# Key-padding mask in the attention scores: part of it moved from a TensorE product to a GpSimd word product

## The chip, the cores and the metric

One core of a Trainium2 chip runs the whole program. The number that counts is device time in microseconds (us) of one execution. TensorE is called PE here, VectorE DVE, ScalarE ACT, GpSimd POOL; the DMA queue of SyncE is SP.

## What is computed

The input is `x` of 8 sequences of 512 tokens by 256 features. Three residual blocks follow each other. The first is a bidirectional Mamba with a feed-forward. The second, the one that matters here, is cross attention with 16 heads of 16 features over 512 keys, of which the last ones are padding and are masked for every query. The third is a feed-forward whose result goes through five steps of a spiking neuron.

```python
scores = jnp.einsum('bhqd,bhkd->bhqk', q, k) / math.sqrt(D_HEAD)
scores = jnp.where(mask == 0, jnp.float32(-1000000000.0), scores)
attn = jax.nn.softmax(scores, axis=-1)
out = jnp.einsum('bhqk,bhkd->bhqd', attn, v)
...
y = jnp.einsum('bsf,df->bsd', h, W_proj)
def step(mem, _):
    reset = jax.lax.stop_gradient(spike_fn(mem - THRESHOLD))
    mem_new = BETA * mem + y - reset * THRESHOLD
```

## The kernel before

There are two passes. `mamba_pass` takes the first 1700 us or so and is not touched by the change. `attention_pass` then goes through the eight sequences (batches), and each engine has its own program, written out by hand, with semaphores between them. What stands in one engine's program stays in that order.

One batch on PE is, in this order: the first half of the feed-forward of the next batch (`up`, `down`) interleaved with `prescore` (scores whose maximum per query DVE takes, the line of `masked`); then the attention proper; then key, value, output and query projections; then the spiking feed-forward (`fc`, `spike_input`).

The attention proper works with transposed scores: keys lie on partitions, queries along the free axis. It has eight **units** (0 to 7). Unit `u` is a group of four heads (`g = u // 2`) and two of the four key tiles (`2s` and `2s + 1` with `s = u % 2`). A unit has two **halves**, each with two heads. `score(b, unit, half)` makes, for each of its two heads and each of the unit's two key tiles, two bf16 products of 512 columns into one PSUM bank: `k_st` by `q_st` (L1411 and L1412), and then `ident_bf` by `mask_biasT`, which adds minus 2^32 to the scores of the padded keys. So a half has eight products. The two banks of a head form a `pair` tile, of which there are two, so a head waits for the exponential of the head two places earlier. ACT takes the exponential of a pair, 128 by 1024, into `pr`. `weigh(b, unit, half)` multiplies one key tile of `pr` of four heads by `v_sb` (with a column of ones, for the softmax sum); half 0 takes key tile `2s`, half 1 takes key tile `2s + 1`. PE's order is

```python
for unit in range(H // 2):
    for half in range(2):
        if unit + 1 < H // 2:
            score(b, unit + 1, half)
        weigh(b, unit, half, it)
    if unit % 2 == 0 and unit > 0:
        to_tokens(unit // 2 - 1, it)
```

with `score(b, 0, 0)` and `score(b, 0, 1)` ahead of the loop. In the traces a weigh reads as eight MATMUL records (each fp32 product is two), and `to_tokens` is the transposes from `oT` at L1435.

Meanwhile DVE adds the feed-forward's result to `x1n` (L1671), runs the five spike steps of the batch before (`cnt`, `tmp`, `mem`, 128 by 1024 fp32, L1718 to L1737), with the query norm of the next batch between step 1 and step 2 (statistics L1635 and L1642, application L1649), and after each `to_tokens` a `normalise` (L1702, L1706). POOL's program in a batch is short: `x1n` sums, the cutting of the maxima into three bf16 parts (L1892 to L1898), `rstd_of` of the query norm and of the later norm (L1863, L1865), another sum. It has nothing to do during the attention's units.

Of the kernel before, what the change touches and what calls it, by code (L numbers as in the profile page):

```python
# [11 lines left out]
B, T, D = 8, 512, 256  # L12
DI, NS, RK, CW = 512, 16, 16, 4
FF = 1024
H, DH = 16, 16
P = 128
# [6 lines left out]
QR = 6 * DH + 3  # L23
# [17 lines left out]
_cols()  # L41


Q_PART = [0, 0, 1, 0, 2, 1]
K_PART = [0, 1, 0, 2, 0, 1]

# [1057 lines left out]
def attention_pass(nc, ctx, a, mid, out, sb, where, stage, psum, consts, handover, early):  # L1104

    f32, bf16, i32 = mybir.dt.float32, mybir.dt.bfloat16, mybir.dt.int32
    ALU, ACT, AX = mybir.AluOpType, mybir.ActivationFunctionType, mybir.AxisListType
    ident, cols, minus_half, col, settle, s_const = consts
    pair, bank, y_bank, general = psum
# [26 lines left out]
    v_sb = sb("v_sb", [P, TT, H, 32])  # L1136
    qk = sb("qk", [P, 2, KD, T])
    qk_part = sb("qk_part", [P, 2, 3, KD, T], bf16)
    oT = sb("oT", [P, 2, T])
    m_col = sb("m_col", [P, TT, H])  # L1140
    m_part = sb("m_part", [H // 2, 2, 3, T], bf16)
    m_rest = sb("m_rest", [H // 2, T])
# [53 lines left out]
    m_cut = stage("m_cut", ahead=1)  # L1196
    s_sc = stage("score")
    s_exp = stage("exp", ahead=2)
    g_out = stage("g_out")
    out_ready = stage("out_ready")  # L1200

    with nc.Block() as block:
# [96 lines left out]
        def _(pe):  # L1299
            pe.wait_ge(handover.sem, handover.count(0))  # L1300

            def mm(o, lhsT, rhs, start=True, stop=True):
                return pe.matmul(o, lhsT, rhs, start=start, stop=stop)  # L1303
# [96 lines left out]
            def score(b, unit, half):  # L1400

                g, s = unit // 2, unit % 2
                if unit == H // 4 and half == 0:
                    pe.wait_ge(s_mr[1].sem, s_mr[1].count(b))
                for hh in (2 * half, 2 * half + 1):
                    hd = 4 * g + hh
                    n = b * 2 * H + unit * 4 + hh
                    pe.wait_ge(s_exp.sem, s_exp.count(n - 2))
                    for t in range(2):
                        kt = 2 * s + t  # L1410
                        mm(pair[hh % 2][:, t, :], k_st[0:QR, hd, kt * P:(kt + 1) * P], q_st[0:QR, hd, :], True, False)  # L1411
                        last = mm(pair[hh % 2][:, t, :], ident_bf[:, :], mask_biasT[:, kt, :], False, True)  # L1412
                    last.then_inc(s_sc.sem, 1)

            def weigh(b, unit, half, it):

                g, s = unit // 2, unit % 2
                pe.wait_ge(s_exp.sem, s_exp.count(b * 2 * H + unit * 4 + 3))
                key = ("av", g)
                if s == 0 and half == 0:  # L1420
                    pe.wait_ge(*G.free(key, it))
                bk = G.bank(key, it)
                kt = 2 * s + half
                for hh in range(4):
                    last = mm(bk[32 * hh:32 * hh + 32, :], v_sb[:, kt, 4 * g + hh, :], pr[:, hh, kt, :],
                              kt == 0, kt == TT - 1)
                if kt == TT - 1:
                    last.then_inc(G.full_sem(key), 1)
# [195 lines left out]
        def _(dve):  # L1624
# [6 lines left out]
            def norm_stats(n, src):  # L1631

                dve.drain()
                for j in range(TT):
                    dve.bn_stats(stats[:, j, :], src[:, j, :])  # L1635
                norm_mean(n)
# [28 lines left out]
            def add_down(beta, it):  # L1665

                dve.wait_ge(x1n_set.sem, x1n_set.count(beta))
                for jj in range(TT // 2):
                    dve.wait_ge(*G.full(("w2", jj), it))
                    bk = G.bank(("w2", jj), it)  # L1670
                    dve.tensor_tensor(two(x1n, jj), two(x1n, jj), bank_tiles(bk), ALU.add).then_inc(G.done_sem(("w2", jj)), 1)  # L1671
# [17 lines left out]
            def take_q(it):  # L1689
                for m in range(KD):  # L1690
                    dve.wait_ge(*G.full(("q", m), it))
                    bk = G.bank(("q", m), it)
                    dve.scalar_tensor_tensor(qk[:, 1, m, :], bk[:, :], col("bq", m), not_full[:, :],
                                                              ALU.add, ALU.mult).then_inc(G.done_sem(("q", m)), 1)
# [63 lines left out]
            for jj in range(TT // 2):  # L1758
                take_v(jj, BEFORE)
            dve.drain()  # L1760
            dve.tensor_tensor(mask_biasT[:, :, :], keep[:, :, :],
                              not_full[:, :].unsqueeze(1).broadcast_to((P, TT, T)), ALU.mult)
            take_q(BEFORE)
            cut_lo(0, 1)
            cut_last(0, 1)
# [18 lines left out]
            def batch(b, it, more):  # L1784
# [7 lines left out]
                start, step, finish = spikes(b)  # L1792
                if more:
                    add_down(b + 1, it)
                start()
                step(1)
                if more:
                    norm_stats(ATT, x1n)
                    norm_apply(ATT, b + 1, x1n, xn_q)
                step(2)  # L1800
                normalise(0, it)
# [54 lines left out]
        def _(pool):  # L1856
# [47 lines left out]
            rstd_of(FF1, 1)  # L1904
            take_x1(0)

            def batch(b, more):
                if more:
                    start_x1n(b + 1)
                for i in range(2):  # L1910
                    cut_maxima(b, i)
                if more:
                    rstd_of(ATT, b + 1)
                rstd_of(FF2, b)
                if more:
                    pool.wait_ge(kinds["wo"][1].sem, kinds["wo"][1].count(2 * b + 1))
                    take_x1(b + 1)
                    rstd_of(FF1, b + 2)
# [131 lines left out]
```

## Time and profile before

| | us |
|---|---|
| median of 3 runs | 2940.82 (2939.02 to 2941.04) |
| the profiled execution's own time | 2934.87 |
| its span in the trace | 2933.1 |
| PE busy | 2739.0 (93%) |
| PE weight loads busy | 1812.9 (62%) |
| DVE busy | 2189.3 (75%) |
| ACT busy | 1757.3 (60%) |
| POOL busy | 1554.4 (53%) |

The shares mix two passes. The page's 40 slices show them apart: up to about 1700 us POOL is busy at 80 to 90%, afterwards at 10 to 20%, while PE stays at 90% or more. Matmul records overlap, so a busy PE says only that it had work in hand; how fast it goes is read from the starts of its records.

### The profile page before, as it was taken

Reading aid. Unit: us, or ns where it says so; the run is one execution under the profiler, and the core shown is the slowest. Engines: PE = TensorE matmul, PEld = TensorE weight load, DVE = VectorE, ACT = ScalarE, POOL = GpSimd, SP = SyncE. Lnnn points to the kernel's source line nnn. Section 1 sums busy time; section 2 is a strip of 40 time slices with the busy share of each in tenths; the row PEclk is TensorE's granted clock in tenths of the full one; section 3 lists DMA queues with packets and bytes.
Section 4 is the critical chain, followed back from the end, with each engine's and each line's share of the span. In section 5 each row is a group of like instructions: output and inputs, shape, how many; then the busy total and the mean of one; then the engine's idle time right before and its main releaser. Section 6 shows DMA issues by size and latency. Waiting matters only on the chain. (4 is left out here: it accounts for less than half of the span.)

```text
span 2933.1 us, 55353 instructions
## 1 busy us (share of the span) xinstructions
PE 2739.0 (93%) x19289; PEld 1812.9 (62%) x19330; DVE 2189.3 (75%) x3270; ACT 1757.3 (60%) x2899; POOL 1554.4 (53%) x850
## 2 busy tenths in 40 slices
PE   5999999999999999999999868999999999999996
PEld 2777777777777777777777744454454545454523
DVE  3988888888889888888888857474748484747473
ACT  5778877877877777678778423535344444444332
POOL 1888888888888888888889821111111111111010
PEclk9999999999999999999999989999999999999978
DMA  3122111202211221212122062414140505050400
GB/s 115 31 75 77 59 62 61 98 26 74 83 63 52 75 77 48 73 61 90 34 73 96 8 142 60 67 28 68 27 73 22 83 11 93 2 93 2 79 2 15
DMA packets 113355, 174.50 MB, mean 59 GB/s; under 512 B 15233, under 2 KB 88065, under 8 KB 113057
## 3 DMA queue, kind: packets, MB, share of 16 engines
q1 hardware_dynamic: 113104, 171.34, 22.9%
q8 instruction: 136, 2.23, 0.3%
q14 instruction: 115, 0.93, 0.1%
HBM read 148.38 MB, written 22.94 MB: 58 GB/s over the span
## 5 line engine op out<-in xcount | busy, mean ns | idle before, releaser
L1066 POOL TENSOR_TENSOR hC<-h,C_rep 128x1024 f32<-128x1024 f32 x512 | 1203.8, 2365 | 236.2 <-PE y_bank L538 231.3
L924 DVE TENSOR_TENSOR_SCAN h<-dA,pair 128x512 f32<-128x512 f32 x1024 | 1178.2, 1203 | 159.4 <-PE pair L447 144.6
L677 ACT ACTIVATE dA<-delta,cols 128x511 f32<-128x511 f32 x1024 | 664.6, 710 | 99.5 <-DVE h L924 93.7
L447 PEld LDWEIGHTS pair<-diagB,duT 64*128 64x128 f32 x8192 | 497.8, 187 | 236.3 <-issue 185.0
L447 PE MATMUL pair<-diagB,duT 64*128 64x128 f32 x8192 | 595.9, 285 | 17.9 <-issue 9.0
L538 PE MATMUL y_bank<-ident,hC 128*128 128x128 f32 x4120 | 563.4, 280 | 13.5 <-POOL hC L1066 11.7
L538 PEld LDWEIGHTS y_bank<-ident,hC 128*128 128x128 f32 x4120 | 441.9, 141 | 79.7 <-POOL hC L1066 19.6
L1790 DVE CUSTOM_DVE_ANT_0 masked<-pair,mask_bias 128x512 f32<-128x512 f32 x512 | 321.9, 687 | 27.5 <-PE pair L1303 13.8
L1863 POOL TENSOR_SCALAR rstd<-mv 128x4 f32<-128x4 f32 x24 | 11.6, 484 | 563.7 <-DVE mv L1642 563.7
L1535 ACT ACTIVATE pr<-pair 128x1024 f32<-128x1024 f32 x256 | 248.3, 1021 | 94.1 <-PE pair L1303 84.0
L447 PE MATMUL general<-xnT,w_in 128*128 128x512 f32 x512 | 252.4, 604 | 7.3 <-ACT zs L677 5.1
L1303 PE MATMUL general<-w_down,g 128*128 128x256 f32 x1024 | 232.5, 380 | 2.8 <-DVEq L1627 2.8
L1892 POOL CAST m_part<-m_rest 8x512 bf16<-8x512 f32 x16 | 12.1, 754 | 417.5 <-ACT m_rest L1535 417.5
L1303 PEld LDWEIGHTS general<-w_down,g 128*128 128x128 f32 x1024 | 193.7, 190 | 34.9 <-issue 3.8
L1303 PE MATMUL pair<-q_st,k_st 99*128 99x512 bf16 x512 | 196.4, 384 | 13.6 <-ACT pr L1535 11.1
L1303 PE MATMUL general<-xT,w_up 128*128 128x512 f32 x360 | 184.0, 652 | 5.9 <-ACT xT L1535 5.5
L1303 PE MATMUL pair<-mask_biasT,ident_bf 128*128 128x512 bf16 x472 | 179.7, 381 | 0.0
L1303 PE MATMUL pair<-k_st,q_st 96*128 96x512 bf16 x512 | 150.6, 403 | 17.3 <-DMA q_st<-qk_parts 13.7
L934 DVE SCALAR_TENSOR_TENSOR u<-general,cols,u 128x511 f32<-128x511 f32 (+2 forms) x192 | 141.0, 734 | 26.6 <-ACT u L677 23.2
L1702 DVE RECIPROCAL rsum<-general 128x16 f32<-128x16 f32 x32 | 8.2, 258 | 192.1 <-PE general L1435 192.1
L1303 PEld LDWEIGHTS pair<-q_st,k_st 99*128 99x128 bf16 x512 | 50.2, 98 | 143.5 <-ACT pr L1535 97.8
L1303 PEld LDWEIGHTS general<-xT,w_up 128*128 128x128 f32 x360 | 74.1, 210 | 85.5 <-issue 74.8
(173 smaller groups left out, 3161.1 us busy)
## 6 DMA issues: line engine op xcount, KB each, us to landing
C_rep<-c_rows SPq DMA_DIRECT2D x128, 512.0 KB, 3.7
w_in<-w_in SPq DMA_DIRECT2D x16, 1024.0 KB, 4.9
qk_parts<-qk_part SPq DMA_DIRECT2D x48, 256.0 KB, 2.5
k_st<-qk_parts SPq DMA_DIRECT2D x48, 256.0 KB, 8.9
q_st<-qk_parts SPq DMA_DIRECT2D x48, 256.0 KB, 8.9
x_in<-x SPq DMA_DIRECT2D x18, 512.0 KB, 4.3
w_out<-w_out SPq DMA_DIRECT2D x17, 512.0 KB, 4.4
mid<-x_out SPq DMA_DIRECT2D x9, 512.0 KB, 6.5
```

What stands on the lines that cost most here:

```text
L447: return pe.matmul(o, lhsT, rhs, start=start, stop=stop)
L538: last = pe.matmul(y_bank[:, c * P:(c + 1) * P], hC[:, g % 2, i, c * P:(c + 1) * P], ident[:, :], start=j == 0 and i == 0 and c == 0, stop ...
L677: return act.activation(o, i, fn, **kw)
L924: last = dve.tensor_tensor_scan(h[:, g % 4, i, :], dA[:, g % 4, i, :], dBu[:, i, :], 0.0, ALU.mult, ALU.add)
L934: dve.scalar_tensor_tensor(u[n][:, k, lag:T], raw[:, 0:T - lag], col("fb"[n] + "conv_w", CW * k + CW - 1 - lag), u[n][:, k, lag:T], ALU.mu ...
L1066: pool.tensor_tensor(hC[:, g % 2], h[:, g % 4], C_rep[:, 2 * j:2 * j + 2, :], ALU.mult).then_inc(s_hC.sem, 1)
L1303: return pe.matmul(o, lhsT, rhs, start=start, stop=stop)
L1535: return act.activation(o, i, fn, **kw)
L1702: dve.reciprocal(rsum[:, :, :], o[:, :, :, DH:DH + 1].squeeze(3))
L1790: dve.tensor_tensor_reduce(masked[:, j % 2, :], bank[j], mask_bias[:, j, :], 1.0, FLOOR, ALU.add, ALU.max, m_col[:, j, hd:hd + 1]).then_in ...
L1863: pool.tensor_scalar(rstd[:, :], mv[:, :, 1], EPS, None, ALU.add)
L1892: pool.tensor_copy(high, m_rest[:, :])
```

## The change

For units 1 to 7, the second head of each half (heads 1 and 3 of the group, the table `ON_POOL`) has no mask product in the second of its two key tiles. The exponentials there are then those of unmasked scores. POOL multiplies them afterwards, in place, as 32-bit integer words by `keep_word`, which is 1 for a kept key and 0 for a padded one: one `TENSOR_TENSOR` of 128 by 512 for each half of units 1 to 7, 14 a batch and 112 in all. It waits for the exponential of its head, and `weigh` of half 1 now waits for POOL's second product of its unit in place of the exponential. `keep_word` is made once by DVE, after `mask_biasT`. It takes the place in memory of `oT`, and `oT` becomes the tile `xT[1]`, which is in use only later in a batch. DVE takes the statistics of the query norm before the first spike step and not after step 1, since POOL's `rstd_of` for them stands ahead of its word products.

```diff
+ON_POOL = ((1,), (3,))
...
-    oT = sb("oT", [P, 2, T])
+    oT = xT[1]
+    keep_word = sb("keep_word", [P, 2, T], i32)
...
+                        on_pool = unit > 0 and t == 1 and hh in ON_POOL[half]
+                        last = mm(pair[hh % 2][:, t, :], k_st[0:QR, hd, kt * P:(kt + 1) * P], q_st[0:QR, hd, :], True, on_pool)
+                        if not on_pool:
+                            last = mm(pair[hh % 2][:, t, :], ident_bf[:, :], mask_biasT[:, kt, :], False, True)
...
-                pe.wait_ge(s_exp.sem, s_exp.count(b * 2 * H + unit * 4 + 3))
+                if half == 0 or unit == 0:
+                    pe.wait_ge(s_exp.sem, s_exp.count(b * 2 * H + unit * 4 + 3))
+                else:
+                    pe.wait_ge(s_kept.sem, s_kept.count(b * (H - 2) + unit * 2 - 1))
...
+            dve.drain()
+            dve.tensor_scalar(keep_word[:, :, :], mask_biasT[:, 1::2, :], 0.0, None, ALU.is_equal).then_inc(s_word.sem, 1)
...
                     add_down(b + 1, it)
+                    norm_stats(ATT, x1n)
                 start()
                 step(1)
                 if more:
-                    norm_stats(ATT, x1n)
                     norm_apply(ATT, b + 1, x1n, xn_q)
...
+            def mask_exp(b, unit, half):
+
+                kt = 2 * (unit % 2) + 1
+                heads = ON_POOL[half]
+                pool.wait_ge(s_exp.sem, s_exp.count(b * 2 * H + unit * 4 + heads[-1]))
+                settle(pool)
+                words = pr[:, heads[0]:heads[-1] + 1, kt, :].bitcast(i32)
+                pool.tensor_tensor(words, words, keep_word[:, unit % 2, :].unsqueeze(1).broadcast_to((P, len(heads), T)),
+                                   ALU.mult).then_inc(s_kept.sem, 1)
+
+            pool.wait_ge(s_word.sem, s_word.count(0))
...
                 if more:
                     rstd_of(ATT, b + 1)
+                for unit in range(1, H // 2):
+                    for half in range(2):
+                        mask_exp(b, unit, half)
                 rstd_of(FF2, b)
```

PE, one half: the score of unit 2, half 1 and the weigh of unit 1, half 1 behind it. Before:

```order
L1408 REGISTER_ALU
L1303 MATMUL pair<-q_st,k_st 128x512 [waits exp]
L1303 MATMUL pair<-mask_biasT,ident_bf 128x512
L1303 MATMUL pair<-q_st,k_st 128x512
L1303 MATMUL pair<-mask_biasT,ident_bf 128x512
L1303 MATMUL general<-pr,v_sb 32x512 [waits exp]
L1303 MATMUL general<-pr,v_sb 32x512 x3
```

These rows are the half's second head and the weigh. The same place after:

```order
L1412 REGISTER_ALU
L1307 MATMUL pair<-q_st,k_st 128x512 [waits exp]
L1307 MATMUL pair<-mask_biasT,ident_bf 128x512
L1307 MATMUL pair<-q_st,k_st 128x512
L1427 ISA
L1307 MATMUL general<-pr,v_sb 32x512 [waits masked_exp]
L1307 MATMUL general<-pr,v_sb 32x512 x3
```

The head's second mask product is gone, and the weigh waits for POOL's `masked_exp`, not for ACT's `exp`.

POOL, from the cutting of the second half of the maxima to the rstd of the later norm. Before:

```order
L1896 CAST m_part<-m_rest 8x512
L1898 TENSOR_TENSOR m_part<-m_rest,m_part 8x512
L1863 TENSOR_SCALAR rstd_7300<-mv_7299 128x4 [waits ln1_stats]
L1865 TENSOR_TENSOR rstd_7300<-rstd_7300,minus_half 128x4
L1861 REGISTER_ALU
L1863 TENSOR_SCALAR rstd_7300<-mv_7299 128x4 [waits ln2_stats]
```

After, where the pair of rows from L1922 on stands 14 times:

```order
L1907 CAST m_part<-m_rest 8x512
L1909 TENSOR_TENSOR m_part<-m_rest,m_part 8x512
L1874 TENSOR_SCALAR rstd_7300<-mv_7299 128x4 [waits ln1_stats]
L1876 TENSOR_TENSOR rstd_7300<-rstd_7300,minus_half 128x4
L1922 ISA
L1925 TENSOR_TENSOR pr<-pr,keep_word 128x512 [waits exp]
```

The word products stand between the two norms' rstd.

DVE, from the sum into `x1n` to the query norm's application. Before:

```order
L1671 TENSOR_TENSOR x1n<-x1n,general 128x512 [waits w2_full]
L1718 TENSOR_SCALAR cnt<-y_sb 128x1024 [waits out_dma]
L1724 SCALAR_TENSOR_TENSOR tmp<-y_sb 128x1024
L1726 SCALAR_TENSOR_TENSOR mem<-y_sb,tmp 128x1024
L1732 SCALAR_TENSOR_TENSOR cnt<-mem,cnt 128x1024
L1635 BN_STATS stats_7298<-x1n 128x6 x4
L1642 BN_AGGR mv_7299<-stats_7298 128x2 x4
L1649 TENSOR_SCALAR xn_q<-x1n,mv_7299,rstd_7300 128x256 [waits ln1_rstd]
```

After:

```order
L1680 TENSOR_TENSOR x1n<-x1n,general 128x512 [waits w2_full]
L1644 BN_STATS stats_7298<-x1n 128x6 x4
L1651 BN_AGGR mv_7299<-stats_7298 128x2 x4
L1727 TENSOR_SCALAR cnt<-y_sb 128x1024 [waits out_dma]
L1733 SCALAR_TENSOR_TENSOR tmp<-y_sb 128x1024
L1735 SCALAR_TENSOR_TENSOR mem<-y_sb,tmp 128x1024
L1741 SCALAR_TENSOR_TENSOR cnt<-mem,cnt 128x1024
L1658 TENSOR_SCALAR xn_q<-x1n,mv_7299,rstd_7300 128x256 [waits ln1_rstd]
```

The statistics have moved ahead of the four instructions of the spike steps.

## Rows read from the trace of the kernel before

**Rows 1.** The page: busy tenths of an engine in 40 slices of the span

```profile
PE   5999999999999999999999868999999999999996
...
POOL 1888888888888888888889821111111111111010
```

**Rows 2.** Groups by line, PE, 1800 to 2933: count, busy, mean ns, idle before

```profile
L1303 PE MATMUL pair<-mask_biasT,ident_bf 128*128 128x512 bf16 x472 | 179.7, 381 | 0.0
```

**Rows 3.** Timeline, second batch, units 1 to 3: start, duration, engine

```profile
1969.98 0.39 PE L1303 MATMUL pair<-q_st,k_st 99*128 99x512 bf16 x1
1970.20 0.38 PE L1303 MATMUL pair<-mask_biasT,ident_bf 128*128 128x512 bf16 x1
...
1971.06 1.94 ACT L1535 ACTIVATE pr<-pair 128x1024 f32<-128x1024 f32 x2 [0.91 <-PE pair L1303]
...
1971.52 0.38 PE L1303 MATMUL pair<-mask_biasT,ident_bf 128*128 128x512 bf16 x1
...
1971.82 1.06 PE L1303 MATMUL general<-pr,v_sb 128*32 128x512 f32 x8
...
1977.52 1.07 PE L1303 MATMUL y_bank<-pr,v_sb 128*32 128x512 f32 x8
```

**Rows 4.** Timeline, second batch, the first scores of unit 1

```profile
1962.31 0.10 PEld L1303 LDWEIGHTS pair<-q_st,k_st 99*128 99x128 bf16 x1 [0.37 <-ACT pr L1535]
...
1962.47 1.94 ACT L1535 ACTIVATE pr<-pair 128x1024 f32<-128x1024 f32 x2 [0.22 <-PE pair L1303]
```

**Rows 5.** Timeline, second batch, POOL and DVE: alone, and side by side

```profile
1938.60 1.15 POOL L1894 TENSOR_TENSOR m_rest<-m_rest,m_part 8x512 f32<-8x512 f32 x1
1939.88 0.60 POOL L1896 CAST m_part<-m_rest 8x512 bf16<-8x512 f32 x1
...
1958.09 1.95 POOL L1894 TENSOR_TENSOR m_rest<-m_rest,m_part 8x512 f32<-8x512 f32 x1
...
1959.11 2.01 DVE L1726 SCALAR_TENSOR_TENSOR mem<-y_sb,tmp 128x1024 f32<-128x1024 f32 x1
...
1969.02 1.23 DVE L1730 SCALAR_TENSOR_TENSOR mem<-mem,tmp 128x1024 f32<-128x1024 f32 x1
```

**Rows 6.** Groups by line, POOL, 1750 to 2933

```profile
L1875 POOL TENSOR_TENSOR x1n<-x_in,x_mid 128x1024 f32<-128x1024 f32 x7 | 16.5, 2351 | 4.3 <-issue 4.3
```

**Rows 7.** Timeline, second batch, from the last scores to the key projection

```profile
1999.40 0.39 PE L1303 MATMUL pair<-q_st,k_st 99*128 99x512 bf16 x1
...
2000.48 1.94 ACT L1535 ACTIVATE pr<-pair 128x1024 f32<-128x1024 f32 x2 [0.91 <-PE pair L1303]
...
2002.83 1.92 PE L1303 MATMUL y_bank<-pr,v_sb 128*32 128x512 f32 x16
...
2004.69 0.30 PEld L1303 LDWEIGHTS general<-ctxT,w_att 128*128 128x128 f32 x2 [0.84 <-issue]
```

**Rows 8.** Timeline, second batch, DVE between the transposes; ACT's key projection

```profile
1991.07 0.26 DVE L1702 RECIPROCAL rsum<-general 128x16 f32<-128x16 f32 x1 [6.74 <-PE general L1435]
...
1996.01 1.23 DVE L1737 SCALAR_TENSOR_TENSOR tmp<-cnt,x_res 128x1024 f32<-128x1024 f32 x1
...
2002.94 0.26 DVE L1702 RECIPROCAL rsum<-general 128x16 f32<-128x16 f32 x1 [5.70 <-PE general L1435]
...
2006.71 0.69 ACT L1535 ACTIVATE qk<-general,cols 128x512 f32<-128x512 f32 x1 [1.29 <-PE general L1303]
```

**Rows 9.** Timeline, before the first batch, DVE: what follows the mask tile

```profile
1734.01 0.75 DVE L1693 SCALAR_TENSOR_TENSOR qk<-general,cols,not_full 128x512 f32<-128x512 f32 x1 [0.39 <-PE general L1303]
1736.19 0.75 DVE L1693 SCALAR_TENSOR_TENSOR qk<-general,cols,not_full 128x512 f32<-128x512 f32 x1 [1.44 <-PE general L1303]
```

**Rows 10.** Stretches of 10 us; the number before the DMA share is PE's clock

```profile
2020.00:2030.00 10.00, 6.55 (x16) 2.88 (x15) 5.35 (x7) 1.60 (x3) 2.62 (x2) 0.75 0.93 163
2030.00:2040.00 10.00, 10.00 (x23) 4.29 (x22) 4.24 (x10) 8.33 (x13) 0.00 (x0) 0.91 0.80 110
...
2170.00:2180.00 10.00, 9.31 (x21) 4.13 (x21) 2.48 (x3) 5.91 (x10) 0.00 (x0) 0.83 1.15 126
```

More of the change, by code:

```diff
@@ L1198, in attention_pass @@
     s_exp = stage("exp", ahead=2)
+    s_kept = stage("masked_exp")
+    s_word = stage("mask_words")
     g_out = stage("g_out")
@@ L1410, in score @@
                         kt = 2 * s + t
-                        mm(pair[hh % 2][:, t, :], k_st[0:QR, hd, kt * P:(kt + 1) * P], q_st[0:QR, hd, :], True, False)
-                        last = mm(pair[hh % 2][:, t, :], ident_bf[:, :], mask_biasT[:, kt, :], False, True)
+                        on_pool = unit > 0 and t == 1 and hh in ON_POOL[half]
+                        last = mm(pair[hh % 2][:, t, :], k_st[0:QR, hd, kt * P:(kt + 1) * P], q_st[0:QR, hd, :], True, on_pool)
+                        if not on_pool:
+                            last = mm(pair[hh % 2][:, t, :], ident_bf[:, :], mask_biasT[:, kt, :], False, True)
                     last.then_inc(s_sc.sem, 1)
```

## The prediction

> **What bounds the kernel now.** I read the page's slices first. After the Mamba pass PE is busy at nine tenths while POOL falls to one tenth [rows 1]. That suggests that PE sets the pace and POOL is free, but busy shares do not prove it, so I went to the timeline of one batch. There the attention's halves follow each other without a hole on PE. In [rows 3] weighs start at 1971.82 and, two halves later, at 1977.52: a half takes 2.85 us. The scores ahead of the first of them start at 1969.98, so 1.84 of it are eight products, and 1.01 the weigh. ACT needs 1.94 us for the two exponentials of a half and stands idle 0.91 until PE has given it a new pair [rows 3]. So PE is the bound, and ACT has room. The eight batches go alike, unit for unit.
>
> The price of one mask product must be read from starts. From 1970.20 to 1971.52 six products start, 0.22 us apart [rows 3], while the same records read 381 ns each [rows 2], because they overlap. Taken at 381 ns, 112 products would be 43 us; at the pitch they are 24.6. I use the pitch. The Trainium skill says the same (Trainium Kernel Development and Optimization, Performance Expectations): matmul busy time is a poor metric, since matmuls are pipelined. That sentence excludes the sum of 43, and the trace agrees.
>
> **What is removed.** 14 mask products a batch, 112 in all: 112 x 0.22 = 24.6 us, if all of it lies on the path. In the steady halves it does: each half goes from 2.85 to 2.63 us. Can ACT follow? A half's first head keeps its four products, so its exponential still starts 1.08 us after the scores (1971.06 less 1969.98), and the pair ends at +3.02. The next half's first head needs the first exponential, ended near +2.10, at +2.63. Its second head comes at +3.51 and needs the second, ended at +3.02. 0.5 us are left, so ACT does not become the bound. In unit 1 PE does wait for exponentials: the fourth head's end releases the second head of unit 1 at 1962.31 [rows 4]. But what is taken away there comes behind that wait and directly ahead of the next weigh, and the first head, whose products start the exponential of 1962.47, keeps all four. So it counts too.
>
> **What is added on POOL.** 14 products a batch of 128 by 512 words. No integer product is in the trace. The nearest rows are two-input operations: 2.35 us for 128 by 1024 fp32 [rows 6], so half, 1.18, for 512; and 1.15 for 8 by 512 when DVE leaves POOL alone [rows 5]. A lower bound is the 0.60 of a one-input cast of 512 [rows 5]; an upper one is 2.35, as if a word cost what two floats cost. I take 1.18, as the two-input rows agree on it whatever their type in or out.
>
> POOL must be ready for the weigh of half 1. Take the scores that start at 1969.98 (unit 2, half 1). Their exponentials end at 1973.00, and the weigh that reads the second key tile starts at 1977.52 [rows 3], 4.52 us later. Three products fewer lie before it now, so 3.86. POOL needs some 0.16 to start, 1.18 to run and 0.05 to release PE: 1.4. This is hidden, with 2.5 to spare. Only one POOL product falls in each 2.63 us, so it keeps pace.
>
> At the **end of unit 7** there is no next score to hide behind. The last scores start at 1999.40, call it S, and the exponentials end at 2002.42, S + 3.02. The two last weighs start at 2002.83 and take 1.86 together until 2004.69 [rows 7], the second at half of that. With one product fewer the first starts at S + 3.21 and the second would at S + 4.14. POOL is done at 3.02 + 1.4 = S + 4.42. PE waits 0.28 a batch, 8 x 0.28 = 2.2 us. With a POOL product of 0.60 this is nothing; with 2.35 it is 1.45 a batch, 11.6 in all.
>
> **DVE and POOL disturb each other.** Side by side, POOL's 1.15 becomes 1.95 and DVE's 1.23 becomes 2.01 [rows 5]; each row reads as if one had stood still until the other was done. The Trainium skill has that as a rule (SBUF — State Buffer, two separate sides): the port pair is an exclusive lock, and a DVE operation with two SBUF inputs and a GpSimd one that reads SBUF exclude each other. So a word product can wait up to 1.23 for a spike step: 1.4 + 1.23 = 2.6 of the 3.86 us, still hidden. The other way round, about four word products fall between two transposes of the outputs and can hold DVE up by 4 x 1.18 = 4.7 us; that stretch also becomes 0.9 shorter. DVE was idle 6.74 and 5.70 us before its two later reciprocals [rows 8], so 5.6 still fits, barely. Its last step of a batch, 1996.01 to 1997.24, would end at worst near 2002, still ahead of the last word product (near 2002.6 on the old scale), so I leave that one undisturbed. The ACT work that waits for that step's DMA starts at 2006.71 [rows 8], 9.5 us after the step, against a delay of 4.7 and a DMA of 512 KB. Cost: nothing.
>
> **The statistics' move** costs nothing. It adds no instruction on DVE, only an order, and the spike steps that come later by it have the idle time just named behind them. POOL's rstd then waits for POOL's own cutting of the maxima alone. Of the cutting, two operations of at most 1.95 are left when the one of 1958.09 ends at 1960.04 [rows 5]; with 2 us for the rstd, an estimate from the same rows for two operations, POOL is free by 1966. The first word product's exponential ends at 1964.41 [rows 4], and the weigh that wants it and the next one was at 1971.82 and is now near 1970.9. Two word products at 2.6 fit ahead of that, if DVE disturbs no more than one of them fully. What follows on POOL's queue, the later norm's rstd, waits for the output projection, which comes behind the last weigh anyway. SP's queue keeps its order. PE's new wait brings one register instruction for each weigh of half 1, hidden while its array works.
>
> **keep_word**, once: 128 by 1024 on DVE, up to 1.2 us after a drain, behind the mask tile. DVE's next instruction starts at 1734.01 after a wait of 0.39, the one behind it, at 1736.19, waits 1.44 for PE [rows 9]. With 1.2 us from 1733.77 on, the first ends at 1735.7, before the second can start. The size of 1.2 is from the spike steps, 1.23 for 128 by 1024 [rows 5]. Cost 0; uncovered, it would be 1.2.
>
> **The sum.** 24.6 - 2.2 = 22.4 us. The profiled execution took 2934.87, and would take 2912.5. The median of the runs, 2940.82, lies 6 above it; I carry the difference over: **2918.4 us**.
>
> **PE's clock** adds noise. After each attention PE idles for the later norm and then shows half clock, 1.2 instead of 2.4 GHz, for a while. In the stretches of 10 us the loss is 0.25 + 0.09 of 10 us, 3.4, in one batch, and 0.17, 1.7, in the next [rows 10]. Five of eight batches show the long form, three the short. As the batch gets shorter, which batches draw which may change: 5 us more if all were long, 8.5 less if all were short. I allow 4 either way.
>
> **Rivals.**
> (a) *The last word product is late*, either since an integer product costs more (1.6 to 2.6 us) or since DVE still holds it up by 1.23. For it: no integer row, and a margin on DVE of only half a microsecond. Against: the steady two-input rows. 1.2 us a batch, 9.6 in all: 2928. The skill's GPSIMD Engine Reference (When to use GPSIMD) says that only a 32-bit integer add has a native path and that the ordinary one computes in fp32; by that the product would go at the fp32 rate and this rival falls. No row here shows it.
> (b) *POOL becomes the bound, slower than before.* 14 products with a gap of 0.15 must fit between the first exponential, near 1964.6, and the last weigh, near 2003.8: 39.2 us, 2.8 each. From 2.65 us a product on, the kernel loses. At 3.0 it is 14 x 3.15 = 44.1, so 4.9 a batch and 39 in all: 2980. Nothing in the rows goes as slowly.
> (c) *The products come off but the halves stay at 2.84*, because the wait of a head for the exponential two places back decides after all. This would need 0.5 us more in that loop than the rows show: 2941.
>
> **How the numbers follow.** Forecast 0.70; (a) 0.14; (b) 0.07; (c) 0.04; 0.05 for a gain above the 24.6, by the clock. The range goes from 2911 (all 24.6 gained, nearly all of it with 4 to 5 us of clock) to 2931 (rival (a) with a worse clock). A measurement of this kernel can tell about 0.2%, 6 us, from no change. Faster by more 0.88, within 0.05, slower 0.07.
>
> **What would show it.** In the changed kernel the starts of weighs in the steady halves lie 2.63 apart; POOL shows 112 word products of about 1.2 us, some near 2 beside a spike step; ACT's idle time before a pair falls from 0.91 to about 0.7; the last weigh waits about 0.3 us for POOL. From the first pair of exponentials of unit 1 to the last pair of unit 7 (1962.47 to 2000.48) it is 38.0 us now; 13 products fewer lie between, so it should be 35.2. Wrong would be: word products above 2.6 us, weighs of half 1 that wait for POOL in every unit, or a gap that grows behind the attention.

## The result, and the profile after

The changed kernel took 2918.03 us (median of 4 runs, 2916.24 to 2921.48) beside 2939.92 of the kernel before (4 runs, 2938.96 to 2941.04). By the medians that is 21.9 us faster. The ratio is 0.9927, with a 95% interval of 0.9912 to 0.9941, or 17 to 26 us. Forecast were 2918.4 us, 22.4 us faster. The profiled execution took 2919.11 us, with a span of 2917.3.

The page of after shows POOL's slices, which answer to [rows 1], and two groups by line (operation, shapes, count | busy us, mean ns | idle before):

```profile
POOL 1788888888888888888889821323232322223130
...
L1544 ACT ACTIVATE pr<-pair 128x1024 f32<-128x1024 f32 x256 | 248.4, 1021 | 72.4 <-PE pair L1307 72.1
...
L1925 POOL TENSOR_TENSOR pr<-pr,keep_word 128x512 int32<-128x512 int32 x112 | 156.4, 1396 | 131.3 <-ACT pr L1544 128.2
```

POOL has gone from one tenth to two or three in the attention. It spends nearly as long waiting for exponentials (128.2 us) as at work (156.4): it keeps up.

The next view is the timeline of the second batch of after (start, duration, engine), unit 1 to unit 3; it answers to [rows 3] and [rows 4]:

```profile
1964.07 1.94 ACT L1544 ACTIVATE pr<-pair 128x1024 f32<-128x1024 f32 x2 [0.22 <-PE pair L1307]
...
1967.28 1.28 POOL L1925 TENSOR_TENSOR pr<-pr,keep_word 128x512 int32<-128x512 int32 x1 [0.41 <-issue]
...
1972.54 1.07 PE L1307 MATMUL general<-pr,v_sb 128*32 128x512 f32 x8
...
1975.16 1.07 PE L1307 MATMUL y_bank<-pr,v_sb 128*32 128x512 f32 x8
...
1977.24 1.94 ACT L1544 ACTIVATE pr<-pair 128x1024 f32<-128x1024 f32 x2 [0.69 <-PE pair L1307]
...
1977.79 1.06 PE L1307 MATMUL y_bank<-pr,v_sb 128*32 128x512 f32 x8
```

Weighs start at 1972.54, 1975.16 and 1977.79: a half now takes 2.62 to 2.63 us where it took 2.85. ACT's idle time ahead of a pair is 0.69 where it was 0.91. Both differences are 0.22, one mask product.

The end of the same batch, which answers to [rows 7] and [rows 8]:

```profile
1990.47 0.26 DVE L1711 RECIPROCAL rsum<-general 128x16 f32<-128x16 f32 x1 [5.21 <-PE general L1444]
...
1993.46 1.71 POOL L1925 TENSOR_TENSOR pr<-pr,keep_word 128x512 int32<-128x512 int32 x1 [1.84 <-ACT pr L1544]
1994.11 2.14 DVE L1741 SCALAR_TENSOR_TENSOR cnt<-mem,cnt 128x1024 f32<-128x1024 f32 x1
...
1999.22 1.94 ACT L1544 ACTIVATE pr<-pair 128x1024 f32<-128x1024 f32 x2 [0.68 <-PE pair L1307]
...
2001.34 1.28 POOL L1925 TENSOR_TENSOR pr<-pr,keep_word 128x512 int32<-128x512 int32 x1 [1.35 <-ACT pr L1544]
2001.36 1.06 PE L1307 MATMUL y_bank<-pr,v_sb 128*32 128x512 f32 x8
2001.46 0.26 DVE L1711 RECIPROCAL rsum<-general 128x16 f32<-128x16 f32 x1 [3.00 <-PE general L1444]
...
2002.67 1.07 PE L1307 MATMUL y_bank<-pr,v_sb 128*32 128x512 f32 x8 [0.25 <-POOL pr L1925]
2003.67 1.99 PE L1307 MATMUL general<-ctxT,w_att 128*128 128x512 f32 x4
```

The last two weighs were one piece of 16 products in [rows 7], the second half of it 0.88 after the first. They are two pieces now, 1.31 apart (2001.36 and 2002.67). The profile's waits of PE name no other wait for POOL than this one (us in all, times, longest):

```profile
PE y_bank L1307 <- POOL pr L1925: 2.0, 8, 0.3
```

From the first pair of exponentials of unit 1 to the key projection it was 1962.47 to 2004.69, 42.22 us. Now it is 1964.07 to 2003.67, 39.60, so 2.62 less. The first seven batches agree in this to 0.01 us. The last batch, which no other follows, went from 43.32 to 40.51, 2.81 less. The eight together give 21.1 us, and the runs gave 21.9.

**The two profiles taken alone would mislead.** The changed kernel's profiled execution was only 15.8 us shorter (2934.87 to 2919.11). Part of the rest was lost before the first batch. The first exponential of each, before and then after:

```profile
1814.40 1.94 ACT L1535 ACTIVATE pr<-pair 128x1024 f32<-128x1024 f32 x2
```

```profile
1817.26 1.02 ACT L1544 ACTIVATE pr<-pair 128x1024 f32<-128x1024 f32 x1
```

The change touches none of PE's work there, but PE's granted clock differs. The stretch from 40 to 60 us of before and of after (the number before the DMA share is the clock):

```profile
40.00:60.00 20.00, 11.31 (x37) 5.26 (x35) 0.69 (x1) 16.78 (x40) 5.76 (x5) 0.89 0.62 216
```

```profile
40.00:60.00 20.00, 13.50 (x37) 6.13 (x35) 0.69 (x1) 15.49 (x35) 4.46 (x4) 0.74 0.60 215
```

The same 37 pieces of PE's work take 13.50 us in place of 11.31. Behind the attentions the low stretch comes in a short and a long form, 1.7 and 3.4 us lost ([rows 10]). Of the seven that another batch follows, before's profile has four long ones, after's five. So 21.1 - 2.9 - 1.7 = 16.5 us were to be expected between the two profiles. The spread within one kernel goes with the clock too: before's own runs on all the chips used here went from 2932.64 to 2942.98 us, and among the fifteen beside run 1 the fastest (2932.64) had a mean granted clock of 0.974 and the slowest (2942.5) one of 0.970. So below I compare medians for the total, and the same place of the same batch for a term.

### The profile page after: what moved, and what is told of

Same layout as the page of the kernel before. It is cut to its first block and busy times, and to the rows that moved or that the text cites. A ratio compares the mean times of both kernels' runs of the same rounds, so it can differ in the third digit from the quotient of the medians.

```text
span 2917.3 us, 55510 instructions
## 1 busy us (share of the span) xinstructions
PE 2722.2 (93%) x19185; PEld 1803.6 (62%) x19218; DVE 2231.5 (76%) x3271; ACT 1755.7 (60%) x2899; POOL 1710.4 (59%) x962
## 5 line engine op out<-in xcount | busy, mean ns | idle before, releaser
L1925 POOL TENSOR_TENSOR pr<-pr,keep_word 128x512 int32<-128x512 int32 x112 | 156.4, 1396 | 131.3 <-ACT pr L1544 128.2
L935 DVE SCALAR_TENSOR_TENSOR u<-general,cols,u 128x511 f32<-128x511 f32 (+2 forms) x192 | 141.1, 735 | 26.1 <-ACT u L678 22.7
L1307 PE MATMUL pair<-mask_biasT,ident_bf 128*128 128x512 bf16 x368 | 140.1, 381 | 0.0
```

The lines of the kernel that those rows point to most:

```text
L935: dve.scalar_tensor_tensor(u[n][:, k, lag:T], raw[:, 0:T - lag], col("fb"[n] + "conv_w", CW * k + CW - 1 - lag), u[n][:, k, lag:T], ALU.mu ...
L1925: pool.tensor_tensor(words, words, keep_word[:, unit % 2, :].unsqueeze(1).broadcast_to((P, len(heads), T)), ALU.mult).then_inc(s_kept.sem, 1)
```

## Experiments

All edits are against the changed kernel. A "tail" is the distance of the last two weighs of a batch, 0.88 before and 1.31 after. "Attention" is the time from the start of a batch's first exponential to the start of its last weigh's last matmul: 46.01 before, 43.40 after, in each of the first seven batches. The last batch is told apart where it matters, since it differs even between two traces of one kernel (43.52 in after's, 44.32 in run 11's).

**1. The removal alone.** The word products are left out, and the weigh waits for the exponential again; so part of the mask is missing from the result. This run shows what the 112 products were worth without any cost.

```diff
-                if half == 0 or unit == 0:
-                    pe.wait_ge(s_exp.sem, s_exp.count(b * 2 * H + unit * 4 + 3))
-                else:
-                    pe.wait_ge(s_kept.sem, s_kept.count(b * (H - 2) + unit * 2 - 1))
+                pe.wait_ge(s_exp.sem, s_exp.count(b * 2 * H + unit * 4 + 3))
...
-                for unit in range(1, H // 2):
-                    for half in range(2):
-                        mask_exp(b, unit, half)
```

> The changed kernel without the word products on GpSimd: the 112 mask products are gone, nothing zeroes the padded keys in their place (that part of the mask is left out of the computation), and the weigh of half 1 waits for the exponential again. My theory, in which removed products lie wholly on TensorE's path at 0.22 us and the only cost of the word products is the wait at the last weigh (0.3 to 0.4 us a batch): 24.6 us below the kernel before, 2915 us, and 3 below the changed kernel. The rival, in which the word products also cost time by holding VectorE up or by a wait in other units: more than 5 us below the changed kernel, 2912 or less.

Measured: 2915.57 us (2912.66 to 2917.4), ratio 0.992 (0.9907 to 0.9934), with before at 2938.26 beside it: 22.7 us, of the 24.6 forecast for the products, which lie within the interval. Attention is 42.94 us, and 46.01 less 14 x 0.22 is 42.93: the other parts of the change (the place of `oT`, `keep_word`, DVE's new order), which this run has too, leave no mark there. In its trace the two last weighs are one piece again:

```profile
1999.26 1.92 PE L1307 MATMUL y_bank<-pr,v_sb 128*32 128x512 f32 x16
2001.12 1.98 PE L1307 MATMUL general<-ctxT,w_att 128*128 128x512 f32 x4
```

The steady halves are 2.63 here, as with the word products. What POOL's part costs is the tail and nothing else that the trace shows. The timing alone could not tell it, since this run's interval and the changed kernel's overlap.

**2. POOL's part alone.** All mask products stay, the word products run too.

```diff
-                        on_pool = unit > 0 and t == 1 and hh in ON_POOL[half]
+                        on_pool = False
```

> The changed kernel with all mask products kept on TensorE, so the word products multiply what is zero already, and nothing is taken away. My theory: only the wait at the last weigh is left. With the half's eighth product there the last weigh but one starts 0.22 us later and covers more of it, so 0.1 to 0.2 us a batch: 2940 to 2942 us, no change against before. The rival (VectorE held up, with work behind it): over 6 us slower, 2946 or more.

Measured: 2943.26 us (2938.43 to 2945.67), ratio 1.0013 (1.0004 to 1.0022). The end of the second batch:

```profile
2009.37 1.28 POOL L1925 TENSOR_TENSOR pr<-pr,keep_word 128x512 int32<-128x512 int32 x1 [1.57 <-ACT pr L1544]
2009.60 2.17 PE L1307 MATMUL y_bank<-pr,v_sb 128*32 128x512 f32 x16
2010.70 0.16 PEld L1307 LDWEIGHTS y_bank<-pr,v_sb 128*32 128x32 f32 x8 [0.94 <-POOL pr L1925]
```

The tail is 1.10, 0.22 over before and 0.21 under after: the mask product that stands ahead of the first weigh here delays it by 0.22 and covers that much of POOL's time. Eight tails are 1.8 us; the ratio gives 3.8 (1.2 to 6.5). By the medians it is 5.0 us, where 0 to 2 was expected. The lower end of the interval lies beneath the trace's value, so a cost beyond the tail is neither shown nor excluded here.

**3. The statistics back behind step 1.**

```diff
                     add_down(b + 1, it)
-                    norm_stats(ATT, x1n)
                 start()
                 step(1)
                 if more:
+                    norm_stats(ATT, x1n)
                     norm_apply(ATT, b + 1, x1n, xn_q)
```

> The changed kernel with the query norm's statistics back behind the first spike step. My theory: GpSimd gets to its first two word products about 1 us later, and the second one was done 2.4 us before its weigh, so no difference to the changed kernel: 2918 us, within 1.5. The rival (the statistics had to come first): the weigh of unit 1, half 1 waits for GpSimd, 1 us or more a batch, 2926 us or more.

Measured: 2917.58 us (2914.17 to 2919.71), ratio 0.9925, the same as after. POOL's rstd is ready 0.9 us later, as expected (8.05 us after the batch's first exponential began, where it was 7.13), and the first two word products run back to back behind it, with the usual single wait of PE at the batch's end:

```profile
1967.73 2.55 POOL L1925 TENSOR_TENSOR pr<-pr,keep_word 128x512 int32<-128x512 int32 x2 [0.41 <-ACT pr L1544]
```

The move of the statistics is worth nothing in time. POOL stays ahead either way.

**4. Another head in half 1.** The word product of the last half is done on head 2, whose exponential is the first of its pair, and no longer on head 3.

```diff
-ON_POOL = ((1,), (3,))
+ON_POOL = ((1,), (2,))
```

> The changed kernel with the table at ((1,), (2,)): in half 1 the first of the two heads, not the second, goes without its mask product. The same number of products, but the word product follows an exponential that ends 1 us earlier. My theory: the wait of the last weigh for GpSimd (0.4 us a batch) goes away, all else stays: 2914.8 us, 3.2 below the changed kernel. The rival (that wait hides another limit, the transposes' bank or the exponential itself): no difference, 2918 us.

Measured: 2915.84 us (2909.77 to 2918.79), ratio 0.9925 (0.9911 to 0.9938). In its trace:

```profile
1994.14 1.28 POOL L1925 TENSOR_TENSOR pr<-pr,keep_word 128x512 int32<-128x512 int32 x1 [0.23 <-ACT pr L1544]
1995.28 1.92 PE L1307 MATMUL y_bank<-pr,v_sb 128*32 128x512 f32 x16
1997.14 1.98 PE L1307 MATMUL general<-ctxT,w_att 128*128 128x512 f32 x4
```

POOL ends at 1995.42, just after the first weigh's start and well ahead of the second's. PE's wait for POOL is gone, the tail is 0.88, and attention is 42.92 us, as in run 1. That is 0.48 less than after in each of the first seven batches, 3.8 us in all if the last one gives as much. The timing showed only 2.2 us between the medians, and hardly any difference between the two ratios (0.9925 and 0.9927), so it was taken again below (runs 10 and 11).

**5. Three heads of four.** 168 mask products off instead of 112. Here half 0 hands two heads to POOL as one operation of 128 by 1024 words.

```diff
-ON_POOL = ((1,), (3,))
+ON_POOL = ((0, 1), (2,))
```

> The changed kernel with the table at ((0, 1), (2,)): in half 0 both heads go without the second mask product and GpSimd zeroes 128 by 1024 words, in half 1 the first head alone. 56 products fewer again. TensorE alone would win 12.3 us by that and 3.4 by the last weigh's wait: 2902 us (rival: nothing but TensorE counts). My theory has GpSimd's 3.8 us a unit and VectorE's spike steps exclude each other, so that GpSimd ends each batch late by up to 4 us: between 2903 and 2925, 2908 likeliest, with waits of TensorE for GpSimd in units 5 to 7.

Measured: 2924.83 us (2924.07 to 2926.62), ratio 0.9949 (0.9936 to 0.9963), at the upper end of what was expected and 17 us above the value held likeliest, and 7 us slower than after although 56 products more are gone. The same end of the second batch:

```profile
1989.06 10.57 POOL L1925 TENSOR_TENSOR pr<-pr,keep_word 128x1024 int32<-128x1024 int32 x4 [0.47 <-ACT pr L1544]
1989.74 3.24 DVE L1739 SCALAR_TENSOR_TENSOR mem<-mem,tmp 128x1024 f32<-128x1024 f32 x1
...
1995.27 3.24 DVE L1746 SCALAR_TENSOR_TENSOR tmp<-cnt,x_res 128x1024 f32<-128x1024 f32 x1
...
1999.68 1.07 PE L1307 MATMUL y_bank<-pr,v_sb 128*32 128x512 f32 x8 [1.90 <-POOL pr L1925]
```

Its steady halves are 2.62 and 2.41, so the products do pay. But a row of four POOL operations (two of 1024 words and two of 512) runs without a pause, 10.57 us, and spike steps of 1.23 stretch to 2.14 or, beside a long operation, 3.24. POOL falls behind there and has not caught up at the end. Only the last weigh waits for it, not those of units 5 and 6 as was expected too. It waits 1.90 us and the tail is 2.96, so the attention takes 43.7 us, 0.3 more than in after.

The rest is clock. In four of the eight batches PE's clock falls right behind this wait, ahead of the idle time in which it falls anyhow. In the first three batches the stretch behind the tail had full clock; here is the fifth's (clock 0.83), where the last weigh started at 2430.08:

```profile
2430.00:2440.00 10.00, 9.92 (x43) 5.58 (x44) 2.26 (x8) 3.96 (x6) 0.03 (x1) 0.83 0.15 52
```

In three of them the last weigh itself runs slower by it, so the attention takes 43.9 us; over the eight batches it is 3.1 us more than in after. Between batches all seven add up to the long form, and one loses 5.1 us. That is 5.1 us more than in after's profile.

**6. All four heads.** 224 mask products off, POOL at 128 by 1024 words in every half.

```diff
-ON_POOL = ((1,), (3,))
+ON_POOL = ((0, 1), (2, 3))
```

> The changed kernel with the table at ((0, 1), (2, 3)): both heads of each half go without the second mask product, and each word product is 128 by 1024. 112 products fewer on TensorE, 24.6 us, which the rival (TensorE stays the bound) gives as 2893 us. My theory: a word product takes 2.5 us, and 14 of them with gaps and VectorE's steps between them take some 43 us where TensorE needs 34, so GpSimd is the bound: 7 us a batch more than the changed kernel, 2975 us, from 2940 (no contention) to 2990.

Measured: 2986.41 us (2985.09 to 2990.15), ratio 1.0157 (1.0143 to 1.0171). This is rival (b), made true. POOL's operations on `keep_word` (count: shortest/median/longest in ns), the timeline, and PE's waits:

```profile
L1925 POOL TENSOR_TENSOR pr<-pr,keep_word x112: 2334/3323/3344, 1824.4 to 2917.2; 128x1024 int32<-128x1024 int32 x112
```

```profile
1983.84 18.88 POOL L1925 TENSOR_TENSOR pr<-pr,keep_word 128x1024 int32<-128x1024 int32 x6
...
1987.42 3.22 DVE L1739 SCALAR_TENSOR_TENSOR mem<-mem,tmp 128x1024 f32<-128x1024 f32 x1
```

```profile
PE y_bank L1307 <- POOL pr L1925: 45.7, 24, 3.9
PE general L1307 <- POOL pr L1925: 22.9, 17, 1.7
```

Undisturbed, a product of this size takes 2.33 us and would just fit into a half, which has two mask products less than before here and takes 2.41 where nothing waits (run 5). With DVE beside it the median is 3.32, about 1 us more, and PE waits 69 us in all. The Trainium skill has the rule behind the two rows (SBUF — State Buffer, two separate sides): the port pair is an exclusive lock held for the whole instruction, and the loser blocks. The trace agrees nearly: the two engines take turns, and each needs 3.2 to 3.3 us, close to its own work and the other's together (2.33 and 1.23, 3.56).

**7. The products of after, each made twice.** A product with a word of 0 or 1 can be repeated without changing anything.

```diff
-                pool.tensor_tensor(words, words, keep_word[:, unit % 2, :].unsqueeze(1).broadcast_to((P, len(heads), T)),
-                                   ALU.mult).then_inc(s_kept.sem, 1)
+                by = keep_word[:, unit % 2, :].unsqueeze(1).broadcast_to((P, len(heads), T))
+                pool.tensor_tensor(words, words, by, ALU.mult)
+                pool.drain()
+                pool.tensor_tensor(words, words, by, ALU.mult).then_inc(s_kept.sem, 1)
```

> The changed kernel with every word product issued twice, the second time without effect on the data. TensorE has the same work as in the changed kernel. This measures the price at which GpSimd becomes the bound. 14 times 2.7 us is 38 us, against 36.8 that the weighs leave: without contention 26 us more than the changed kernel, 2944. My theory adds VectorE's steps, which can go in between any two products: 2960 to 2990 us, and within 15 of the kernel with both heads on GpSimd, though that one has 112 products fewer on TensorE.

Measured: 3013.84 us (3005.16 to 3014.54), ratio 1.0239 (1.0225 to 1.0253). Slower, as rival (b) says, but 24 us above the range expected and 27 above run 6, whose POOL does the same number of words. Lines of POOL in its second batch, L1926 the first and L1928 the second product of a pair:

```profile
1986.02 2.25 POOL L1926 TENSOR_TENSOR pr<-pr,keep_word 128x512 int32<-128x512 int32 x1
1988.42 2.08 POOL L1928 TENSOR_TENSOR pr<-pr,keep_word 128x512 int32<-128x512 int32 x1
1990.45 2.24 POOL L1926 TENSOR_TENSOR pr<-pr,keep_word 128x512 int32<-128x512 int32 x1
...
1994.06 1.28 POOL L1926 TENSOR_TENSOR pr<-pr,keep_word 128x512 int32<-128x512 int32 x1
1995.48 1.27 POOL L1928 TENSOR_TENSOR pr<-pr,keep_word 128x512 int32<-128x512 int32 x1
1996.71 1.28 POOL L1926 TENSOR_TENSOR pr<-pr,keep_word 128x512 int32<-128x512 int32 x1
```

The next product starts 1.2 to 1.4 us behind an undisturbed one, and 2.0 to 2.4 behind a disturbed one. An undisturbed pair takes 2.65 us from start to start (1994.06 to 1996.71), against 2.33 for run 6's one long product: 0.32 more, 4.5 in a batch's 14. That is already more than the 3.4 us a batch (27 in eight) by which this run lies above run 6. DVE does not add to it: in the second batch ten products are held up in either run, for 8.9 us in all here and 10.2 in run 6. So the distance to run 6 is the price of two instructions for one, with the drain between them. What I had underpriced is DVE's part in both. My sum without it was 2944, and 8 x 8.9 = 71 us on top make 3015.

**8. Unit 0 as well.** 16 products a batch instead of 14.

```diff
-                        on_pool = unit > 0 and t == 1 and hh in ON_POOL[half]
+                        on_pool = t == 1 and hh in ON_POOL[half]
...
-                if half == 0 or unit == 0:
+                if half == 0:
...
-                    pe.wait_ge(s_kept.sem, s_kept.count(b * (H - 2) + unit * 2 - 1))
+                    pe.wait_ge(s_kept.sem, s_kept.count(b * H + unit * 2 + 1))
...
-                for unit in range(1, H // 2):
+                for unit in range(H // 2):
```

> The changed kernel with unit 0 treated like the others: 16 products fewer on TensorE, 3.5 us, and 16 word products more. My theory: GpSimd still has the maxima and the norm's rstd ahead of it and begins its first word product near 2.6 us before it could end the second one, so the weigh of unit 0, half 1 waits 2.7 us a batch: 2936 us, from 2932 to 2940. The rival (GpSimd is in time there too): 2915.

Measured: 2950.35 us (2947.72 to 2952.71), ratio 1.0036 (1.0023 to 1.005): 10 us above the range. The fourth batch in its trace, the waits, and the stretch of 10 us with the fourth batch's wait in it:

```profile
2258.26 3.81 POOL L1925 TENSOR_TENSOR pr<-pr,keep_word 128x512 int32<-128x512 int32 x3 [0.40 <-issue]
...
2260.84 1.83 PE L1307 MATMUL general<-pr,v_sb 128*32 128x512 f32 x8 [2.51 <-POOL pr L1925]
```

```profile
PE general L1307 <- POOL pr L1925: 20.2, 8, 2.7
```

```profile
2254.00:2264.00 10.00, 7.49 (x34) 1.97 (x35) 8.90 (x7) 4.70 (x5) 8.52 (x7) 0.85 0.02 5
```

The wait is there as foreseen (2.5 us for an expected 2.7): POOL is busy with the maxima and the rstd when unit 0 wants it. What I had not foreseen is the clock. In six of eight batches the weigh behind the wait runs at half clock (1.83 us here for what took 1.07). Attention is 45.98 us in a batch without the fall and 47.4 to 47.8 in one with it. So six falls cost some 9.5 us, which is nearly all of the miss. That unit 0 was kept apart matters; the place of the statistics (run 3) does not.

**9. Mixed.** Two heads in half 0 for units 1 to 5, where there is time to catch up, one for units 6 and 7; head 2 in every half 1. 152 mask products off.

```diff
-ON_POOL = ((1,), (3,))
+def on_pool_of(unit, half):
+    return ((0, 1) if unit < 6 else (1,), (2,))[half]
...
```

> The kernel with three heads of a unit on GpSimd (0 and 1 in half 0, 2 in half 1), but in units 6 and 7 only heads 1 and 2. In that kernel no half before the last waited for GpSimd, and the last weigh started 2.96 us after the one before it instead of 0.88. My theory, in which GpSimd falls behind by its and VectorE's exclusive use and two words products of half the size near the end let it catch up: the last weigh comes within 0.3 us of 0.88, 19 products a batch are gone, 4.2 us against 3.1, so 8 to 9 us below the kernel with ((1,), (2,)): 2907 us. The rival (GpSimd is late all the same): 2915 or more.

Measured: 2905.71 us (2903.91 to 2906.88), ratio 0.989 (0.9875 to 0.9905), beside 2937.79 for before. It beats both kernels. The products alone would give 152 x 0.22 = 33.4 us; the runs give 32.1. Attention is 42.04 us, PE waits for POOL nowhere, and the two last weighs are one piece again:

```profile
1996.38 1.92 PE L1312 MATMUL y_bank<-pr,v_sb 128*32 128x512 f32 x16
1998.23 1.98 PE L1312 MATMUL general<-ctxT,w_att 128*128 128x512 f32 x4
```

Against run 5 two products a batch are given back, and the wait of 1.90 us is gone. What run 5 lacked was the time to catch up behind unit 5.

**10 and 11. Run 4 and the changed kernel once more**, on one chip with run 9.

> The kernel with ((1,), (2,)) once more, beside the changed kernel on one chip. By the trace it has 0.43 us a batch less of wait, 3.5 us in all: 2914.5 us, 3 to 4 below the changed kernel. The rival: a difference that the clock's draw hides, within 2 us.

> The changed kernel once more, beside the two others on one chip: 2918 us, a ratio of 0.9925 to the kernel before.

Measured: 2916.66 (2914.84 to 2919.02), ratio 0.9927 (0.9914 to 0.9941), and 2919.2 (2917.16 to 2920.65), ratio 0.9933 (0.992 to 0.9947). The other head is 2.5 us better, where the traces say 3.8 and 3 to 4 were expected; the first time it was 2.2, by medians of two separate comparisons. The intervals overlap, so the timing alone does not prove it; two differences of the same sign and the lost wait speak for it. Run 11 is also a second measurement of the change itself: 18.6 us (2937.79 less 2919.2), where the first gave 21.9.

By attention, run 9 should be 8 x 0.88 = 7.0 us below run 10; 8 to 9 were expected, and it is 11.0. The clock behind the attention differs between their profiles, the same stretch of run 9 and of run 10:

```profile
2010.00:2030.00 20.00, 16.54 (x44) 7.88 (x43) 10.16 (x17) 8.03 (x13) 4.37 (x3) 0.91 0.83 118
```

```profile
2010.00:2030.00 20.00, 16.55 (x43) 8.21 (x42) 10.01 (x18) 5.66 (x9) 4.37 (x3) 0.83 0.77 110
```

In run 9's profile all seven of these stretches are short, in run 10's four are long, 4 x 1.7 = 6.8 us. So the clock can hold the missing 4 us. Whether the timing of run 9 favours the short form, or drew it by chance, stays open.

## Why the prediction was right, point by point

- **PE is the bound, ACT has room.** Right. The halves went from 2.85 to 2.63, and ACT still idles 0.69 before a pair, as forecast (about 0.7). Rival (c) falls.
- **0.22 us a mask product, all on the path.** Right. First pair of unit 1 to last pair of unit 7: forecast 35.2, measured 1964.07 to 1999.22, 35.15. With 381 ns a product it would have been some 33. Run 1 gives 22.7 us in all for 112 products, 9 the better version 32.1 for 152: 0.20 and 0.21 each.
- **1.18 us a word product.** Somewhat low: 1.26 at the least and 1.28 in the median. The two-input rows were the right neighbours, 8% short. It goes at the rate of floats: 2.33 us for 128 by 1024 words in run 6, and 2.35 for as many floats in [rows 6]. The Trainium skill (GPSIMD Engine Reference, When to use GPSIMD) says that the ordinary elementwise path computes in fp32 and names a native path for the 32-bit integer add. It gives no time for an integer product; these two durations fit its going by the fp32 path.
- **The tail, 0.28 us a batch.** The mechanism was right and its size off: 0.43 a batch, 3.5 us in all instead of 2.2. Of the 0.15 that lack, 0.10 is the word product, and 0.05 is that I put the second weigh at half of 1.86, 0.93, where it starts 0.88 after the first. The profile names only 0.25 of it as PE's wait, because its count begins where the first weigh's records end. The distance of the starts, 1.31 less 0.88, gives it all. Runs 1 and 4 take the cost away, run 2 shows it without the gain.
- **DVE and POOL disturb each other, hidden.** Right in the form: 1.28 becomes up to 2.18 on POOL, 1.23 becomes 2.14 on DVE. DVE's idle time before its two later reciprocals fell from 6.74 and 5.70 to 5.21 and 3.00, so at most 2.7 of the 5.6 that I had allowed was used; before the first it fell by 3.3 (7.66 to 4.34). What I had not counted is the norm's application, operations with one large input: its four took 1.38 us before and 3.41 beside POOL, at 1966.91. No wait for DVE became longer at PE.
- **The statistics' move, nothing; keep_word, nothing.** Run 3 shows the first. The second is in the setup of after's trace:

```profile
1736.00 0.69 DVE L1773 TENSOR_SCALAR keep_word<-mask_biasT 128x1024 int32<-128x1024 bf16 x1
1736.61 0.74 DVE L1702 SCALAR_TENSOR_TENSOR qk<-general,cols,not_full 128x512 f32<-128x512 f32 x1
```

  It took 0.69 us, less than the 1.2 I allowed. The instruction behind it came some 0.3 us later for it, and the one behind that still had 1.14 us to wait for PE.
- **Rival (a), 2928.** It needed a loss of 1.2 us a batch; the traces have 0.43. **Rival (b), from 2.65 us a product on.** Run 6, at 3.0 us from start to start in its second batch, and run 7, at 3.3 a pair, cross that line and lose 46 and 74 us; the changed kernel, at 1.40 in the mean, is far from it. What I underpriced is what lies between. One hold-up costs POOL some 1.0 us at most in these batches, but their number grows with how densely POOL works: three of a batch's 14 products in after, ten in run 6.
- **The sum.** 24.6 - 3.5 = 21.1 from the traces' terms, 21.9 measured, 22.4 forecast. The term that was off was the tail, by 1.3 us, within what the clock does. That the total came within half a microsecond is luck: the second measurement of the same two kernels gave 18.6 us (run 11), and the interval is some 9 us wide.

## What to carry to other kernels

When one engine paces a loop, work can be handed to a free engine for as long as it ends before its reader comes. The last pass of the loop decides this, because no further work follows to cover it: choose for it the piece whose input is ready first (head 2, not head 3), and hand over less there than in the middle, as run 9 did. Price one matmul by the distance of starts. Price a shift from or to DVE or POOL by how often the two will then meet, not by their own times alone, and count two short instructions as dearer than one long one even where nothing disturbs them (run 7).

## What the runs showed of the hardware

- POOL and DVE side by side take turns. A POOL product of 128 by 1024 words goes from 2.33 to 3.32 us, and the DVE step beside it, 1.23 alone, to 3.24. DVE operations with one large input are held up too: the four of the norm's application go from 1.38 to 3.41 us beside POOL (before and after, second batch).
- Two POOL products of 512 columns with a drain between them take 2.65 us from start to start, undisturbed (run 7), one of 1024 columns 2.33 (run 6).
- A wait of 2.5 us of PE in the attention's first unit was followed by half clock in six of eight batches (run 8), which cost 1.5 to 1.8 us each. Behind a wait of 1.9 us at the attention's end (run 5) the clock fell in four of eight batches, ahead of the idle time that follows there anyhow. A wait costs more than its own length then. Why some batches have the fall and others not, no run here shows.
- An integer product on POOL takes as long as a two-input floating-point one: 1.26 to 1.28 us for 512 columns, 2.33 for 1024 (floats: 2.35).
- Traces of different executions show different clocks at the start and behind each attention. The same kernel's runs lay up to 10 us apart (2932.64 to 2942.98), the slower ones with the lower granted clock, and two profiles set side by side hid 6 of the 22 us gained.
